# Biases of six linear products: added on GpSimd (POOL) to the evicted tiles instead of by a TensorE matmul

## The reference

```python
# block a, layers 0 and 1
a = softmax(h @ h.T / temper)
attn = a * adj;  attn = attn / (sum(attn) + 1e-10)
hl = h @ wl.T + b_l;  hs = h @ ws.T + b_s;  hr = h @ wr.T + b_r
ctx = (attn * upper) @ hl + diag(attn) * hs + (attn * lower) @ hr
h = relu(norm(ctx))
# block b, layers 2 and 3
m_left, m_right = h @ W_left.T, h @ W_right.T      # no bias
u = (h @ m_left.T, h @ m_right.T, masked) / temper
attention = exp(u) * adj / (sum + 1e-10)
h_lin = h @ W_lin.T + b_lin
ctx = attention @ h_lin
h = relu(norm(ctx))
# block c, layers 4 and 5: two attentions of 12 heads, the first with an output product
```

## Time and profile before

| what | value |
|---|---|
| device time, median of 3 runs (lowest to highest) | 3245.1 us (3242.33 to 3245.72) |
| profiled execution: its time, its span | 3241.71 us, 3240.0 us |
| busy share of the span: PE, PEld, DVE, ACT, POOL | 96%, 74%, 84%, 51%, 15% |
| mean granted TensorE clock | 0.993 |
| first matmul | 86.2 us after the start |

### The profile page before, as it was taken

How to read it: one execution, slowest core, us unless ns; L and a number is a source line. 1 busy time by engine, 2 the same in 40 slices (tenths; PEclk the granted TensorE clock), 3 DMA queues, 4 the chain that set the end, 5 groups by cost and what they waited for, 6 DMA issues and landing times.

```text
span 3240.0 us, 86317 instructions
## 1 busy us (share of the span) xinstructions
PE 3094.3 (96%) x34944; PEld 2413.3 (74%) x34944; DVE 2712.0 (84%) x7670; ACT 1666.2 (51%) x4446; POOL 482.7 (15%) x908
## 2 busy tenths in 40 slices
PE   0799999999999999999999999999999999999996
PEld 0477777777777777777778777777777777777774
DVE  6588888888888888888888888888888888888885
ACT  3255555555555555555555555555555555555553
POOL 1111111111111111111111111111111111111110
PEclk9999999999999999999999999999999999999997
DMA  5000000000000000000000000000000000000000
GB/s 165 7 8 13 13 8 13 13 7 13 13 7 13 13 7 13 13 7 13 13 7 13 13 7 13 13 10 11 13 13 7 13 13 7 13 13 7 13 7 6
DMA packets 36979, 47.73 MB, mean 15 GB/s; under 512 B 3668, under 2 KB 36564, under 8 KB 36584
## 3 DMA queue, kind: packets, MB, share of 16 engines
q1 hardware_dynamic: 36544, 42.15, 4.1%
q10 hardware_dynamic: 40, 0.06, 0.0%
HBM read 29.62 MB, written 12.58 MB: 13 GB/s over the span
## 4 chain that ended last, share of the span: by engine, by line
PE 94%; DVE 2%; ACT 2%; issue 1%; DMA 1%; POOL 0%; ACTq 0%; POOLq 0%; SPq 0%; DVEq 0%
PE bank_a L266 27%; PE bank_c L266 22%; PE bank_b L266 20%; PE bank_c L310 7%; PE bank_b L297 4%; PE bank_c L438 3%; PE bank_b L304 2%; PE bank_b L310 2%; PE bank_c L454 1%; PE bank_c L453 1%; PE bank_c L455 1%; ACT htc_hi L559 1%; PE bank_a L343 1%; PE bank_b L392 1%; PE bank_a L310 1%
## 5 line engine op out<-in xcount | busy, mean ns | idle before, releaser
L573 ACT ACTIVATE prob<-score,neg_head_max 128x128 f32<-128x128 f32 x1536 | 495.0, 393 | 22.4 <-DVE neg_head_max L828 21.8
L266 PE MATMUL bank_c<-htc_hi,w_lo 128*128 128x128 f16 x2304 | 409.0, 219 | 0.0
L266 PE MATMUL bank_c<-htc_hi,w_hi 128*128 128x128 f16 x2304 | 409.0, 219 | 0.0
L266 PE MATMUL bank_c<-htc_lo,w_hi 128*128 128x128 f16 x2304 | 409.0, 219 | 0.0
L266 PE MATMUL bank_a<-w_hi,hta_hi 128*128 128x384 f16 x1152 | 377.0, 328 | 0.0
L266 PE MATMUL bank_a<-w_lo,hta_hi 128*128 128x384 f16 x1152 | 376.9, 327 | 0.0
L823 DVE SCALAR_TENSOR_TENSOR score<-bank_c,bias 128x384 f32<-128x384 f32 x512 | 279.9, 547 | 55.7 <-PE bank_c L438 55.5
L828 DVE TENSOR_REDUCE neg_head_max<-score 128x3 f32<-128x384 f32 x512 | 279.4, 546 | 8.9
L621 DVE SCALAR_TENSOR_TENSOR pt_lo<-bank_c,pt_hi 128x384 f16<-128x384 f32 x512 | 271.2, 550 | 18.6 <-ACT pt_hi L497 18.6
L310 PE MATMUL bank_c<-ident,prob 128*128 128x128 f32 x1536 | 245.1, 276 | 9.5 <-ACT prob L573 9.1
L497 ACT ACTIVATE pt_hi<-bank_c 128x384 f16<-128x384 f32 x512 | 239.9, 482 | 24.9 <-PE bank_c L310 24.9
(11 more groups left out here) (185 smaller groups left out, 8886.4 us busy)
## 6 DMA issues: line engine op xcount, KB each, us to landing
x_in<-x SPq DMA_DIRECT2D x64, 192.0 KB, 2.4
out<-y_out SPq DMA_DIRECT2D x64, 192.0 KB, 2.3
w_stage<-w_t SPq DMA_DIRECT2D x10, 576.0 KB, 5.7
adj_in<-adj SPq DMA_DIRECT2D x64, 64.0 KB, 2.2
score<-w_t SPq DMA_DIRECT2D x5, 576.0 KB, 5.5
prob<-w_t SPq DMA_DIRECT2D x4, 576.0 KB, 7.1
norms<-norm_rows SPq DMA_DIRECT2D x8, 192.0 KB, 5.0
m_sides<-biases ACTq DMA_DIRECT2D x5, 6.0 KB
```

The costliest lines, as they stand in the source:

```text
L266: mm = nc.tensor.matmul(out_ap, a, b, start=first and i == 0, stop=last and i == len(pairs_of) - 1)
L573: ex = nc.scalar.activation(prob[:, j, c, :], score[:, j, c, :], ACT.Exp, bias=neg_head_max[:, j, c:c + 1])
```

## The change

The bias matmul goes from the left, right and linear products of layers 0 to 3 (rows 0, 2, 3, 5, 8 and 11 of `biases`). Their float32 rows are spread over all partitions in `bias_rows_f32` by six DMAs, issued on SP after the fifth weight and ahead of the norm rows. After ACT's copy, POOL adds the row to the tile in place, in two new streams: e (`side_bias`) and f (`lin_bias`). PE's turn of the attention and its next product need only the bank and wait for the copy (`hr_evicted`, `hl_evicted`); PE's context product waits for the sum (`hl_ready`, `hr_ready`, `lin_ready`). The other biases (self products, and block c's) stay on PE, so `bias_hl` shrinks from 20 rows to 8, and from ten pieces to four, each loaded by two small DMAs instead of one. The orders of all four engines are written anew.

```diff
-B_PIECES = (N_W + 1) // 2
+PE_BIASES = (1, 4, 14, 15, 16, 17, 18, 19)
+POOL_BIASES = (0, 2, 3, 5, 8, 11)
+B_PIECES = len(PE_BIASES) // 2
 ORDER = {
-    "pe": "xcxxyybayyyayyyxcbxwbwwccwcwcwccaccadcayyyyyyyyawcbwxxxxcxxxwcbxcwcxbccccbwacwyybaxxxx",
-    "act": "bbcabaccbxccwcppcppwwacacccabcbbcpbwcpcbpwpxbpabbwc",
-    "dve": "aaqacaaabbacabnaaabacccccbcbcbbcbpjpppjjjpjaaaacamaaipiiicainccbccczccpczbbzpbnbppapbbabbp"
-           "bappppbanp",
-    "pool": "aabcanlqbbm",
+    "pe": "ybyaxxcxxxxxacbcxxwcwbwbwcwccwaccwacadyyyyyyyyawcbwxwxcxxxwwcccxxccccbcaxyybxwacbyyyyyy",
+    "act": "bcabbcbccabppxbpcwpwawcacccabcwbpcccpppbbwpbaxbwccc",
+    "dve": "cbnacccccccacbbababppapbbabbpbjjjjpjaacapaaaiaiciimqaicccbccccpczzpppzapnabbpbnbppppanapaa"
+           "cababbabba",
+    "pool": "fbeebaaqelmecfabn",
 }
...
-        bias_hl = sb("bias_hl", [128, N_W + 1, D], f16)
+        bias_hl = sb("bias_hl", [128, len(PE_BIASES), D], f16)
+        bias_rows_f32 = sb("bias_rows_f32", [128, len(POOL_BIASES), D])
...
                 if m == W_STAGES:
+                    for i, m_bias in enumerate(POOL_BIASES):
+                        sp.dma_start(bias_rows_f32[:, i, :], biases[m_bias:m_bias + 1, :].to_broadcast([128, D]))\
+                            .then_inc(bias_rows_loaded, 16)
...
-                ops = [(ones2[:, :], bias_hl[:, m, :])]
+                ops = [(ones2[:, :], bias_hl[:, PE_BIASES.index(m), :])] if m in PE_BIASES else []
...
-                    pe.wait_ge(*hr_ready.at(g, k))
+                    pe.wait_ge(*hr_evicted.at(g, k))
...
                     pe.wait_ge(*attn_ta_ready.at(g, k))
+                    pe.wait_ge(*hl_ready.at(g, k))
+                    pe.wait_ge(*hr_ready.at(g, k))
                     product(a1[:, 0:D], [(attn_ta[:, i, :], sides[:, i, :]) for i in range(2)]).then_inc(ctx_a_done[g], 1)
...
-                    copy(sides[:, 0, :], a0[:, 0:D]).then_inc(hl_ready[g], 1)
+                    copy(sides[:, 0, :], a0[:, 0:D]).then_inc(hl_evicted[g], 1)
...
-                    copy(lin[:, :], b0[:, 0:D]).then_inc(lin_ready[g], 1)
+                    copy(lin[:, :], b0[:, 0:D]).then_inc(lin_evicted[g], 1)
...
+            def side_bias(g):
+                for k in (1, 2):
+                    for i, evicted, ready in ((0, hl_evicted, hl_ready), (1, hr_evicted, hr_ready)):
+                        if g == 0 and (k, i) == (1, 0):
+                            pool.wait_ge(bias_rows_loaded, 16 * len(POOL_BIASES))
+                        pool.wait_ge(*evicted.at(g, k))
+                        P.tensor_tensor(sides[:, i, :], sides[:, i, :], bias_rows_f32[:, 2 * k - 2 + i, :], ALU.add)\
+                            .then_inc(ready[g], 1)
+                        yield
+
+            def lin_bias(g):
+                for k in (1, 2):
+                    pool.wait_ge(*lin_evicted.at(g, k))
+                    P.tensor_tensor(lin[:, :], lin[:, :], bias_rows_f32[:, 3 + k, :], ALU.add).then_inc(lin_ready[g], 1)
+                    yield
```

More of the change, by code:

```diff
@@ L15 @@
 W_STAGES = 4
-B_PIECES = (N_W + 1) // 2
+PE_BIASES = (1, 4, 14, 15, 16, 17, 18, 19)
+POOL_BIASES = (0, 2, 3, 5, 8, 11)
+B_PIECES = len(PE_BIASES) // 2
 ORDER = {
-    "pe": "xcxxyybayyyayyyxcbxwbwwccwcwcwccaccadcayyyyyyyyawcbwxxxxcxxxwcbxcwcxbccccbwacwyybaxxxx",
-    "act": "bbcabaccbxccwcppcppwwacacccabcbbcpbwcpcbpwpxbpabbwc",
-    "dve": "aaqacaaabbacabnaaabacccccbcbcbbcbpjpppjjjpjaaaacamaaipiiicainccbccczccpczbbzpbnbppapbbabbp"
-           "bappppbanp",
-    "pool": "aabcanlqbbm",
+    "pe": "ybyaxxcxxxxxacbcxxwcbwbwcwccwaccwacadyyyyyyyyawcbwxwxcxxxwwcccxxccccbcaxyybxwacbyyyyyy",
+    "act": "bcabbcbccabppxbpcwpwawcacccabcwbpcccpppbbwpbaxbwccc",
+    "dve": "cbnacccccccacbbababppapbbabbpbjjjjpjaacapaaaiaiciimqaicccbccccpczzpppzapnabbpbnbppppanapaa"
+           "cababbabba",
+    "pool": "fbeebaaqelmecfabn",
 }
 FIRST = {
[4 rows of a table removed]
[4 rows of a table added]
 }
@@ L157, in gnn_stack_kernel @@
         hl_done, hr_done, hs_done = Signal("hl_done", 2), Signal("hr_done", 2), Signal("hs_done", 2)
-        hl_ready, hr_ready, self_ready = Signal("hl_ready", 2), Signal("hr_ready", 2), Signal("self_ready", 2)
+        hl_evicted, hr_evicted, self_ready = Signal("hl_evicted", 2), Signal("hr_evicted", 2), Signal("self_ready", 2)
+        hl_ready, hr_ready = Signal("hl_ready", 2), Signal("hr_ready", 2)
         ata_done, attn_ta_ready, ctx_a_done = Signal("ata_done", 2), Signal("attn_ta_ready", 2), Signal("ctx_a_done", 2)
@@ L167, in gnn_stack_kernel @@
         ml_ready, mr_ready, lin_ready = Signal("ml_ready", 2), Signal("mr_ready", 2), Signal("lin_ready", 2)
+        lin_evicted = Signal("lin_evicted", 2)
         ub_done, tri_u_ready, u_sum_ready = Signal("ub_done", 2), Signal("tri_u_ready", 2), Signal("u_sum_ready", 2)
@@ L200, in gnn_stack_kernel @@
         norms_loaded, beta_loaded = sem("norms_loaded"), sem("beta_loaded")
+        bias_rows_loaded = sem("bias_rows_loaded")
         consts_set, consts_ready, dve_consts = sem("consts_set"), sem("consts_ready"), sem("dve_consts")
@@ L285, in columns @@
                 cols = slice(o * 128, (o + 1) * 128)
-                ops = [(bias_hl[:, m, cols], ones2[:, :])] if biased else []
+                ops = [(bias_hl[:, PE_BIASES.index(m), cols], ones2[:, :])] if biased else []
                 for c in range(CHUNKS):
@@ L363, in weight_a @@
                     yield
-                    pe.wait_ge(*hl_ready.at(g, k))
+                    pe.wait_ge(*hl_evicted.at(g, k))
                     rows_first(a0, m + 1, hta_hi)
@@ L516, in weight_a @@
                     act.wait_ge(*hl_done.at(g, k))
-                    copy(sides[:, 0, :], a0[:, 0:D]).then_inc(hl_ready[g], 1)
+                    copy(sides[:, 0, :], a0[:, 0:D]).then_inc(hl_evicted[g], 1)
                     yield
                     act.wait_ge(*hr_done.at(g, k))
-                    copy(sides[:, 1, :], a1[:, 0:D]).then_inc(hr_ready[g], 1)
+                    copy(sides[:, 1, :], a1[:, 0:D]).then_inc(hr_evicted[g], 1)
                     yield
@@ L591, in bias_hi @@
                     act.wait_ge(bias_zeroed, 1)
-                act.wait_ge(b_loaded[piece % 2], 16 * (piece // 2 + 1))
+                act.wait_ge(b_loaded[piece % 2], 32 * (piece // 2 + 1))
                 nc.scalar.activation(bias_hl[0:2, 2 * piece:2 * piece + 2, :], bias_rows(piece), ACT.Copy,
@@ L598, in _ @@
                     act.wait_ge(b_split, piece - 1)
-                act.dma_start(bias_rows(piece), biases[2 * piece:2 * piece + 2, :].unsqueeze(0)
-                              .to_broadcast([2, 2, D])).then_inc(b_loaded[piece % 2], 16)
+                for i in range(2):
+                    m = PE_BIASES[2 * piece + i]
+                    act.dma_start(bias_rows(piece)[:, i, :], biases[m:m + 1, :].to_broadcast([2, D]))\
+                        .then_inc(b_loaded[piece % 2], 16)
                 if piece >= 1:
@@ L994, in stream @@
                     yield from steps(g)
-            woven("pool", n=stream(start_a), l=stream(mask_a), a=stream(roots_a), m=stream(mask_b), b=stream(roots_b),
+            woven("pool", e=stream(side_bias), f=stream(lin_bias), n=stream(start_a), l=stream(mask_a), a=stream(roots_a), m=stream(mask_b), b=stream(roots_b),
                   q=stream(mask_c), c=stream(roots_c))
```

## The result

The kernel after takes 3276.8 us (median of 4 runs, 3276.6 to 3281.7), the kernel before 3243.7 beside it (4 runs, 3241.9 to 3245.7). The ratio is 1.010, with a 95% interval of 1.009 to 1.012: 33 us slower, where 3213 had been forecast. PE lost the matmuls and the idle start about as forecast; the stalls were twice as long as the one I counted.

The account below looks back on a forecast made before the run. PE, busy 96% of the span, was taken as the bound, plus an 86 us start without a matmul. 3241.7 - 62.4 (matmuls) - 22.5 (start) + 2 (first graph) = 3159, + 54 (DVE stall) = 3213 us; range 3165 to 3305.

Parts of the forecast that it names:

- PE's part: Six bias matmuls fewer per graph on PE, 0.1625 us each: 0.975 us per graph, 62.4 us in all.
- The start: Before the first matmul: fewer bias pieces and less zeroing let the weights start earlier; net 22.5 us after extra row loads.
- the first graph's longer chain: Two additions of block a in sequence, uncovered in the first graph: about 2 us more.
- An addition: One POOL addition of 128x384: 1.0 us, the middle between 0.67 and 1.37.
- The direct wait for lin: Block b's context product on PE waits 0.15 us for lin's copy and addition, cancelled by 0.1 us less for `htc_hi`.
- The sum without collisions: Whole kernel if no POOL addition holds up a DVE operation: 3159 us.
- The stall of `x2`: Block b's second context to `node_c`'s turn: hl and hr additions delay DVE's chain, 0.85 us per graph, 54 us.
- Who waits indirectly: Places where a POOL addition holds a DVE operation with two SBUF inputs that decides PE's next start; 54 us counted.
- rival 2: Slower: additions also hold `r_used` (first layer) or make the second `node_c` late behind root c; 51 us each; chance 0.35.

Follow-up runs that it names:

- orders_only: The kernel before, all biases on PE, with the changed kernel's orders on all four engines: 3222.1 us, ratio 0.9935 to the kernel before.
- the narrow additions: The changed kernel with all six POOL additions cut from 384 columns to one, waits and orders kept: 3147.7 us, 0.970 to the kernel before.

## Why the prediction was wrong

Step by step:

- **PE's part**, 62.4 us: right to about a tenth. There are 34,560 matmuls, and from `orders_only` to the narrow additions the distance between neighbouring starts in mid-run falls from 47.88 us (1497.05 to 1544.93) to 47.01 (1451.36 to 1498.37), 0.87 where six matmuls are 0.975.
- **The start**, 22.5 us: right. The first tile waits 64.8 us, 21.4 less. Against it stood 2 us for the first graph's longer chain. The run's end alone (from the last turned adjacency on) grew by 3.5 us, 93.9 to 97.4, of which `orders_only` shows 1.7.
- **An addition**, 1.0 us: right, 0.998 for lin. The sides' mean of 1.077 holds some that DVE held up.
- **The direct wait for lin**, 0.15 us against 0.1 back from `htc_hi`: both sizes off, to the good. The wait for lin is 1.2 us over the whole run, and the one for `htc_hi` fell by 0.25 us per graph (17.6 to 1.9 us in all).
- **The sum without collisions**, 3159: the narrow additions gave 3147.7. The new orders are themselves better by 21 us, which I had not priced; part of that does not show here.
- **The stall of `x2`**: the place and the mechanism right, as the timeline shows. Its price was 54 us, measured 44: two errors that nearly cancel. From the start of the context product (1502.12), hr's addition is over at 4.60 us and `x` at 5.02, 0.68 late, where the working let `x2` only begin at 4.9, 1.1 late. And there was hardly any slack to take off: with narrow additions `node_c` is done at 6.46 and turned by PE at 6.52, where the working had 6.6 and 6.87. (Its own terms add up to 6.4, not 6.6.)
- **The step that failed** is the count under "Who waits indirectly": "The main one is" this one, the other two left to rival 2 at 0.35. Both came: `r_used` and the second `node_c`, 34 and 43 us, where I had 51 for each (both together 3315, not the 3317 written there). All stalls together, less what the orders gained, are 48.99 - (48.16 - 0.975) = 1.80 us per graph instead of 0.85. That is past the 1.3 at which rival 2 decides. 3243.7 - 62.4 - 21.4 + 64 x 1.80 + 2 for the first graph = 3277 us. That the miss is 64 us and not more is luck: with the two stalls at their measured 77 us the forecast would have been 3290; the unpriced gain of the orders and the cheaper `x2` hid the rest.

In detail, at `r_used` my own working gave the answer: addition at 0.25, `r_used` at 0.45, that is 0.20 us apart, and the trace has 0.23. The 0.20 is no coin toss here: `r_used` took 0.80 us in 62 of the 64 graphs. It should have been in the sum. At root c I asked the wrong question. I had looked at whether `diag_a` or the addition goes first, and said that the tiny one first costs nothing. It did go first, in all but three graphs. The next on DVE, `node_c`, was caught instead. The prediction looked only for operations with two SBUF inputs, and `node_c` reads one tensor. The trace of before had the evidence, the same operation beside a mask on POOL (groups, then timelines, of the kernel before):

```profile
L643 DVE TENSOR_SCALAR node_c<-x,mean_var_bc,rstd_bc 128x384 f32<-128x384 f32 x64 | 32.6, 510 | 0.7 <-POOL rstd_bc L925 0.7
L643 DVE TENSOR_SCALAR node_c<-x,mean_var_c,rstd_c 128x384 f32<-128x384 f32 x64 | 30.2, 472 | 0.9 <-POOL rstd_c L925 0.9
```

```profile
1552.59 0.51 DVE L643 TENSOR_SCALAR node_c<-x,mean_var_bc,rstd_bc 128x384 f32<-128x384 f32 x1
...
1552.43 0.46 POOL L954 TENSOR_TENSOR tri_mask<-adj_in,upper_incl 128x128 f32<-128x128 f32 x1
```

The `node_c` that starts 0.16 us into the mask ends 0.21 us after it, as in the kernel after, where it ends 0.22 us after the addition. The mask is so short that this costs 38 ns; beside a 1.0-us addition it costs 0.62.

Two things stay open. From the orders alone to the narrow additions the mean repetition falls by 0.82 us where six matmuls are 0.975. Some 0.05 of the missing 0.15 comes from the first distance, which is longer there (45.6 against 43.6 us); the other 0.1 was not tried. And the three meetings, each released alone, account for 122 of 129 us; whether the other 7 are more than these medians differ by is not shown.

## What to carry to other kernels

Work moved to POOL is priced by its length at every place where DVE's chain decides PE's next start, not by POOL's free time: list each such place, take the start of both operations from the trace, and put every meeting that comes in each graph in the sum. Ask it of the next DVE operation too, not only of the one that starts together, and look in the trace of before for two forms of one operation with slightly different means: 510 against 472 ns was the sign. Where a place has no room, leave that one piece on PE; three or four of six moved beat both all and none.

## What the runs showed of the hardware that was not expected

A DVE operation with one SBUF tensor and [128, 1] scalars, 128x384 float32, is held by POOL as fully as one with two: 0.48 us becomes 1.10, by additions and also by a zeroing that only writes (1.07). It ends about 0.2 us after POOL's instruction, while `r_used`, 0.18 us alone, ends 0.04 after. The Trainium skill (VectorE: DVE Perf Modes, "Mode 2×_2P — use both read ports for one tensor") gives that form both ports when source and destination are in SBUF, also for float32. The trace is in line with it so far as this operation takes 0.48 us where the two-input one of the same size takes 0.56, though that is far from half; no run shows which mode it used.
